# A vision tower with a routed feed-forward layer: the order of the work in the last group of a one-core kernel

## What is computed

```python
h = tokens(x)                                     # patches @ W.T + b, class token, times pos_embed
h = h + attention(layernorm(h))                   # 8 heads, q and k through relu, scores / sum(k)
z = layernorm(layernorm(h)) * ln_scale + ln_bias  # the feed-forward part norms once more
h_shared, h_expert = swiglu(z @ shared_in.T), swiglu(z @ expert_in.T)    # silu(a) * b, 256 wide
g = argmax(z @ group_gate.T + group_bias)         # one of 2 groups of 4 experts
p = softmax(expert logits of group g)             # top 2 of them, weights divided by their sum
out = h + h_shared @ shared_out.T + shared_b \
        + sum_e comb[:, e] * (h_expert @ expert_out[e].T) + cnt @ expert_bias
```

## Time and profile before

| | |
|---|---|
| median of 3 runs | 459.95 us (458.52 to 461.21) |
| the profiled execution | 458.25 us, span 456.4 us |
| TensorE busy | 436.9 us (96%) |
| VectorE, ScalarE, GpSimd busy | 307.0, 190.8, 178.8 us |
| mean granted TensorE clock | 0.994 of full speed |

### The profile page before, as it was taken

The page is one execution under the profiler, slowest core; times in us unless marked ns, Lnnn a source line. Parts: engine busy times, 40 slices in busy tenths (PEclk is TensorE's granted clock), DMA queues, the critical chain, the costliest instruction groups (busy, mean ns, idle before and its releaser), DMA issues.

```text
span 456.4 us, 6968 instructions
## 1 busy us (share of the span) xinstructions
PE 436.9 (96%) x2329; PEld 308.5 (68%) x2329; DVE 307.0 (67%) x895; ACT 190.8 (42%) x362; POOL 178.8 (39%) x217
## 2 busy tenths in 40 slices
PE   6969999899999999999999999999999999999996
PEld 2336455656886677767876588567866778878674
DVE  0152476477766966596848685777678877886686
ACT  1015523753266415742384217632564238522440
POOL 7112721222165316532473127410662254515454
PEclk9999999999999999999999999999999999899999
DMA  8999646134103720074005510360000000010001
GB/s 329 388 405 354 210 158 186 65 116 149 60 1 106 217 70 0 2 250 140 0 1 153 181 55 1 118 201 3 2 13 12 1 1 1 1 25 1 0 2 49
DMA packets 16452, 45.96 MB, mean 101 GB/s; under 512 B 1905, under 2 KB 7585, under 8 KB 16417
## 3 DMA queue, kind: packets, MB, share of 16 engines
q1 hardware_dynamic: 14704, 43.50, 28.2%
q10 hardware_dynamic: 1712, 2.02, 1.3%
HBM read 43.39 MB, written 2.13 MB: 100 GB/s over the span
## 4 chain that ended last, share of the span: by engine, by line
PE 78%; DVE 10%; DMA 4%; issue 4%; POOL 2%; ACTq 1%; ACT 1%; DVEq 0%; POOLq 0%
PE acc L482 22%; PE B L468 5%; PE O L576 5%; DMA bq_row<-in_bq_row 4%; PE scores L702 3%; PE scores L704 3%; PE scores L703 3%; PE C L702 3%; PE scores L546 2%; PE C L704 2%; PE C L703 2%; PE B L525 2%; PE C L634 2%; PE B L511 1%; PE C L635 1%
## 5 line engine op out<-in xcount | busy, mean ns | idle before, releaser
L482 PE MATMUL acc<-x_main,w_patch 128*128 128x512 f32 x288 | 139.4, 607 | 6.0 <-DMA w_patch<-in_w_patch 4.3
L482 PEld LDWEIGHTS acc<-x_main,w_patch 128*128 128x128 f32 x288 | 50.6, 192 | 47.4 <-issue 36.6
L1914 POOL TENSOR_TENSOR prod<-prod 128x512 f32<-128x512 f32 x31 | 39.9, 1287 | 27.6 <-DVE q_nat L1343 10.7
L1002 ACT ACTIVATE probs_t<-B 128x512 f32<-128x512 f32 x32 | 19.0, 595 | 51.5 <-PE B L468 51.5
L576 PEld LDWEIGHTS O<-v_bd,probs_t 128*128 128x128 f32 x256 | 31.9, 192 | 10.4 <-issue 7.6
L1903 POOL TENSOR_TENSOR hidden_lo<-silu,hidden_hi 128x512 fp32r<-128x512 f32 x16 | 20.2, 1268 | 40.8 <-ACT hidden_hi L1002 40.8
L576 PE MATMUL O<-v_bd,probs_t 128*128 128x64 f32 x256 | 31.6, 272 | 0.0
L1845 POOL TENSOR_TENSOR rstd<-var,neg_half 128x4 f32<-128x4 f32 x8 | 8.1, 1017 | 50.8 <-DVE var L1300 50.8
L1002 ACT ACTIVATE probs<-shift 128x512 f32<-128x512 f32 x32 | 20.0, 626 | 18.5 <-DVE shift L1356 16.8
L1002 ACT ACT_TABLE_LOAD x19 | 24.4, 1283 | 7.1 <-issue 6.8
L702 PE MATMUL scores<-w_eout_hi,hidden_hi 128*128 128x512 f32 x64 | 27.3, 426 | 0.0
(11 more groups left out here) (335 smaller groups left out, 1008.0 us busy)
## 6 DMA issues: line engine op xcount, KB each, us to landing
x_main<-in_x_main SPq DMA_DIRECT2D x40, 768.0 KB, 4.4
x_main<-in_x_main SPq DMA_DIRECT2D x8, 512.0 KB, 4.0
x_main<-in_x_main SPq DMA_DIRECT2D x8, 256.0 KB, 3.2
x_tail<-in_x_tail SPq DMA_DIRECT2D x8, 224.0 KB, 4.6
out_tokens<-y_out SPq DMA_DIRECT2D x14, 128.0 KB, 3.1
prod<-in_w_eout SPq DMA_DIRECT2D x2, 512.0 KB, 15.1
w_patch<-in_w_patch ACTq DMA_DIRECT2D x5, 192.0 KB, 10.3
silu<-in_w_in SPq DMA_DIRECT2D x2, 256.0 KB, 13.9
```

The source lines that it names most:

```text
L482: last = mm(acc[:, :], w_patch[:, j, :], x_main[:, j, :], start=(j == 0), stop=False)
L1002: return nc.scalar.activation(dst, src, func, **kw)
L1914: q.tensor_tensor(p[r, 0, :], p[r, 0, :], p[r, 1, :], ALU.add).then_inc(tree1_done.sem, 1)
```

## The change

Four lists are reordered in the last stage; no call is added or taken away.

```diff
             ffn_in(L, 1, TOK)
             expert(L - 1, 6, 128)
             ffn_in(L, 2, TOK)
+            ffn_in(L, 3, TOK)
             expert(L - 1, 7, 128)
             class_out()
-            ffn_in(L, 3, TOK)
             counts(L, TILES, 128)
@@ scalar
             z_out(L, TOK)
-            for k in range(4):
-                silus(L, k, TOK)
-            hidden_high(L, 0, TOK)
-            counts_out(L, TOK)
-            hidden_high(L, 1, TOK)
-            shared_out(L, TOK)
+            silus(L, 0, TOK)
+            silus(L, 1, TOK)
             load_table(L, 3, ACT.Exp)
             route_exp(L, TILES, 128)
+            load_table(L, 4, ACT.Silu)
+            silus(L, 2, TOK)
+            silus(L, 3, TOK)
+            hidden_high(L, 0, TOK)
+            hidden_high(L, 1, TOK)
+            counts_out(L, TOK)
+            shared_out(L, TOK)
             z_out(GROUPS, IMAGES)
-            load_table(L, 4, ACT.Silu)
             for k in range(4):
                 silus(GROUPS, k, IMAGES)
@@ vector
             weigh(L - 1, 5, 128)
+            weigh(L - 1, 6, 128)
             hidden_mul(L, 2, TOK)
-            weigh(L - 1, 6, 128)
+            hidden_mul(L, 3, TOK)
             class_residual()
+            weigh(L - 1, 7, 128)
             norm2(GROUPS, h2_cls, 1, IMAGES)
-            hidden_mul(L, 3, TOK)
+            weights(L, TILES, 128)
             norm2_scale(GROUPS, h2_cls, 1, IMAGES)
-            weigh(L - 1, 7, 128)
-            weights(L, TILES, 128)
             weigh(L, 0, 128)
@@ gpsimd
             expert_sum(L - 1, 2, 128)
-            norm_scale2(GROUPS, 1, IMAGES)
             hidden_low(L, 0, TOK)
             hidden_low(L, 1, TOK)
-            z_low(GROUPS, IMAGES)
+            norm_scale2(GROUPS, 1, IMAGES)
             expert_sum(L - 1, 3, 128)
+            z_low(GROUPS, IMAGES)
             hidden_low(GROUPS, 0, IMAGES)
```

More of the change, by code:

```diff
@@ L1986, in _ @@
             expert_sum(L - 1, 2, 128)
-            norm_scale2(GROUPS, 1, IMAGES)
             hidden_low(L, 0, TOK)
             hidden_low(L, 1, TOK)
+            norm_scale2(GROUPS, 1, IMAGES)
+            expert_sum(L - 1, 3, 128)
             z_low(GROUPS, IMAGES)
-            expert_sum(L - 1, 3, 128)
             hidden_low(GROUPS, 0, IMAGES)
```

## The result

The changed kernel takes 461.62 us (median of 20 runs, 459.25 to 466.08), the kernel before 459.97 (20 runs, 457.31 to 462.92): a ratio of 1.0045, with a 95% interval of 1.0026 to 1.0065. It is slower by 1.65 us, 0.36% by the medians and 0.45% by the ratio. The profiled execution took 459.91 us with a span of 458.1, 1.7 more than before, at nearly the same granted clock (0.996 and 0.994).

The account below looks back on a forecast made before the run. TensorE reaching the end of expert(L,6) was taken to bound the kernel. Transpose delay +1.55 and a vanished wait of -0.1 gave +1.45 us on the 459.95 median: 461.4 us, 8 in 10 within 459.3 to 463.3.

Parts of the forecast that it names:

- What bounds the kernel: At the end: TensorE's expert(L,6) releases it; VectorE's 3.0 us idle before e_keep is not on the path.
- ScalarE: Behind silu(L,1): exponential done at 423.39, 9.9 us earlier; silu(L,2) 0.86 later at 424.81, covered by TensorE's next work.
- The rival with a longer switch: ScalarE's two table switches each drain 1.28 us beyond the load; shared_t(L) comes 1.1 later, 462.5 us; chance 2%.
- TensorE up to expert(L, 0): With ffn_in(L,3) moved ahead, shared_t(L) starts 0.64 earlier at 428.15, expert(L,0) at 430.6, keeping 0.4.
- VectorE and GpSimd hold each other up: Before the class rows' transpose: GpSimd additions hold VectorE, z_cls at 434.1, TensorE waits 1.9 us, +1.55.
- Behind the transpose: TensorE's later work: its wait at counts(GROUPS) disappears, some -0.1; the rest moves with TensorE.
- The holds are missed: VectorE's L1497 slips past GpSimd's addition: +0.55; if norm2 slips through as well, -0.5; chance 15%.
- The clock falls in the wait: TensorE's clock drops after its 1.9 us wait at 432: +3.15, 463.1 us; chance 12%.
- Something late shrinks: In the last stretch VectorE enters earlier; up to 0.5 us comes back, 460.9, or -1.0 with missed holds; chance 9%.
- the forecast case: z_cls late by the hold of VectorE and GpSimd: +0.5 to +2.25, likeliest 461.4 us; chance 62%.

Follow-up runs that it names:

- norm2 ahead: Changed kernel with VectorE's norm2 for the class rows ahead of weigh(L-1,7), and norm2_scale ahead of weights(L): 459.95 us, ratio 0.9984 against the kernel before.
- the sum behind z_low: Changed kernel with GpSimd's expert_sum(L-1,3) put back behind z_low(GROUPS): 458.91 us, ratio 0.9966 against the kernel before.
- the swap alone: Kernel before with only ffn_in(L,3) ahead of expert(L-1,7) on TensorE and hidden_mul(L,3) ahead of class_residual on VectorE: 462.76 us.
- both cures: Changed kernel with norm2, weigh(L-1,7), norm2_scale ahead of weights on VectorE and expert_sum(L-1,3) behind z_low(GROUPS) on GpSimd: 459.94 and 460.11 us.

## Why the prediction was right, and where it was off

The forecast was 461.4 us with 459.3 to 463.3; measured 461.62. The sum was +1.45 on the profiled execution; its span grew by 1.7 and its end stage by 1.67.

- **What bounds the kernel: right.** The end follows expert(L, 6), +2.00 there. VectorE's 3.0 us of idle time were off the path: removing them alone changes the end stage by 0.11.
- **ScalarE: right to 0.03 us.** The exponential ended at 423.41 (predicted 423.39), silu(L, 2) began at 424.84 (424.81). The second load cost TensorE nothing: class_out starts without a wait. The rival with a longer switch fell: the exponential starts 1.40 behind the load, the next silu 1.40 behind the second. The 2.66 us for a switch in the Trainium skill's page "ScalarE: Activation LUTs", section "What ACT_TABLE_LOAD costs", is not seen in either of the two switches.
- **TensorE up to expert(L, 0): right, 0.1 to 0.2 late.** shared_t at 428.24 (428.15), expert(L, 0) at 430.77 (430.6): against silu(L, 1), 0.58 and 0.27 earlier than before, where I had 0.64 and 0.4.
- **VectorE and GpSimd hold each other up: right in kind, 0.6 too small.** z_cls was ready at 434.74 instead of 434.1, TensorE's wait 2.38 instead of 1.9, and the term to the transpose +2.17 instead of +1.55. Up to var2 the replay was within 0.1: 431.22 for 431.14. Held through the second hidden_low was the third of norm2's additions, L1293, and not the step behind it: only two slipped through, which made no difference to the time. The step that failed is the next: "weights(L) begins with it at 431.05, and takes 0.9 us to its L1497: due at 431.95, held to the end of that addition (1.27), 433.03." Held was e_group, the second of the seven, from 431.38 to 433.15. It cost 1.58 us more than its 0.19 unheld, and five steps of weights and norm2_scale still had to follow it. In my pattern the two holds fell on L1497 and L1500; here one long hold came early, and the later instructions were stretched by only 0.1 each. I had the addition's start right (431.84 for 431.76), and counted only what comes due behind that start as held. The pair e_group 1.77 and 0.19 shows that an instruction that comes due beside the root is held already when an addition stands queued behind it.
- **Behind the transpose: the gains were larger than the 0.1.** 0.17 us up to the end of expert(L, 6), and 0.33 behind it, most of it in one row of VectorE's last chain, 0.42 where the same instruction took 0.70 before, because GpSimd's last addition is over by then. Before:

```profile
449.58 0.46 POOL L1921 TENSOR_TENSOR routed<-prod 128x128 f32<-128x128 f32 x1
449.62 0.70 DVE L1549 TENSOR_TENSOR prod<-prod 128x256 f32<-128x256 f32 x1
```

After:

```profile
450.61 0.46 POOL L1923 TENSOR_TENSOR routed<-prod 128x128 f32<-128x128 f32 x1
450.92 0.69 DVE L1536 TENSOR_TENSOR prod<-scores,comb 128x512 f32<-128x512 f32 x1 [0.61 <-PE scores L704]
451.64 0.42 DVE L1551 TENSOR_TENSOR prod<-prod 128x256 f32<-128x256 f32 x1
```

It took 0.42 or 0.43 in the three traces where GpSimd was done (both of the changed kernel, and norm2 ahead), and 0.65 to 0.71 in all nine where it was not.

So +2.17 - 0.17 - 0.33 = +1.67: the total was closer than its terms, since one was 0.6 too small and the other 0.4 too small with the opposite sign. That they cancel to 0.2 is luck. In part so is 461.62 against 461.4, since the interval of the ratio leaves the whole difference between 1.2 and 3.0 us.

- **The rivals.** *The holds are missed:* the holds were there; with the sum behind z_low, where norm2 is held and weights is not, the end stage is 35.29, +0.05 on before. That lies between this rival's two prices, -0.5 and +0.55. *The clock falls in the wait:* it did not in either trace of the changed kernel; the windows behind the wait show 1.00. A mean clock under 0.99 was seen in 14 of 32 executions of the changed kernel and in 33 of 75 of the kernel before, but one of 0.981 or less in 6 and 2. None of those was profiled, so whether the clock fell behind the wait in some of them stays open. *Something late shrinks:* it did, by 0.33, as a correction to the forecast case and not in its place.

**What stays open.** Whether e_group waited from its own start at 431.38 because the addition had in truth begun by then, or because a queued addition claims something earlier than its row shows, these traces can't tell: both fit the 1.77 us. And the rule by which a held instruction gets in between two GpSimd operations is not complete. L1291 in the changed kernel ended at 429.50 between the two hidden_low, and L1306 with norm2 ahead ended at 434.73 between two additions; but in the run with the swap alone L1304, due beside the first hidden_low, was held through both:

```profile
433.26 2.50 DVE L1304 TENSOR_SCALAR x_main<-x_main,mv,rstd 64x128 f32<-64x128 f32 x1 [0.68 <-POOL rstd L1849]
```

## What to carry to other kernels

An engine's longest idle time is worth nothing if the engine that sets the end isn't waiting for what is late there; ask who uses the result, and when. When short VectorE steps on SBUF operands lie on the way to TensorE, look at what GpSimd has queued at that time, not only at what it is running: one 1.3 us addition turned a 0.2 us step into 1.8. Put GpSimd's long sums behind the short steps that others wait for, and let a result that is asked for first be made first, ahead of one that has four us of room.

## What the runs showed of the hardware

- **GpSimd's root did not hold VectorE, the addition behind it did.** e_group, 32 elements from two SBUF inputs, due 0.08 us behind the start of GpSimd's 64x1 root: 0.19 us, or 1.77 with the addition behind the root. The Trainium skill's page "SBUF — State Buffer", section "🔬 SBUF: two separate sides", says that VectorE and GpSimd share a pair of ports as an exclusive lock, which a GpSimd operation that starts first keeps for its whole length against a VectorE operation with two SBUF inputs or in a two-port mode. For the additions and for hidden_low the traces agree (1.23 for a one-element step); for the root they do not, since it too reads SBUF, started first, and held nothing. The Trainium skill's page "Perfetto Trace Analysis", section "GPSIMD Engine Instruction", says to take GpSimd's rows as unreliable in length and to go by their spacing; a hold that begins before the addition's displayed start, at 431.38 against 431.84, would fit that.
- **Held and not held.** Held were tensor_tensor, tensor_scalar and scalar_tensor_tensor on SBUF operands (L1291, L1293 and L1493 in the changed kernel, L1304 and L1497 in the kernel before, L1306 with norm2 ahead). The two TENSOR_REDUCE of weights took 0.19 each in the changed kernel, beside the addition of 433.18 to 433.90.
- **The clock makes the runs spread.** Executions of the changed kernel reached from 459.25 to 466.08 us in the first comparison: 459.25 at a mean clock of 1.00, 461.47 to 462.69 at 0.992, 463.41 to 464.26 at 0.984. The clock is not all of it, for the slowest had 0.985. The windows around 390 us differ from trace to trace of kernels that are the same up to there, as in these of the kernel with both cures, profiled twice. First run:

```profile
392.00:394.00 2.00, 2.00 (x17) 1.80 (x16) 1.03 (x2) 1.41 (x6) 1.89 (x3) 0.50 0.00 0
394.00:396.00 2.00, 2.00 (x16) 1.97 (x14) 1.95 (x4) 0.84 (x2) 0.00 (x0) 0.76 0.00 0
```

Second run:

```profile
392.00:394.00 2.00, 2.00 (x16) 1.77 (x14) 1.73 (x3) 0.08 (x1) 0.65 (x1) 0.50 0.00 0
394.00:396.00 2.00, 2.00 (x12) 2.00 (x11) 1.90 (x5) 1.45 (x4) 0.00 (x0) 0.50 0.01 4
```

The clock stays at its lower level (0.50 of full speed, 1.2 GHz) for longer in the second, whose span is 458.2 against 457.1 with the same end stage. Differences of a few tenths of a us can be read in this kernel only from a stage behind such windows.
